# A cross-attention and mixture-of-experts layer: heads paired on the partitions, maxima added by a product, one ring of banks for the cross attention

## What is computed

```python
x = x + xattn(layernorm(x), ctx)      # 16 heads of 64; softmax kept at its 32 largest of 64 scores
y = layernorm(x)
hn = layernorm(y) * ln1_g + ln1_b
q, k, v = (hn @ w + b for w, b in ((wq, bq), (wk, bk), (wv, bv)))     # 16 heads of 16
attn = softmax(q @ k.T / sqrt(16))                                    # 512 x 512 per head
y2 = y + attn @ v @ wo + bo
hn2 = layernorm(y2) * ln2_g + ln2_b
idx = argmax(hn2 @ gate_w + gate_b)                                   # one of 8 experts
out = x + y2 + relu(hn2 @ w1[idx] + b1[idx]) @ w2[idx] + b2[idx]
```

## Time and profile before

| what | value |
|---|---|
| median of 3 runs | 1525.85 us (1525.6 to 1525.93) |
| the profiled execution's own time | 1527.39 us |
| its span in the trace | 1525.6 us |
| mean granted TensorE clock | 0.936 of full speed |
| PE busy | 1326.6 us, 87% |
| DVE busy | 1080.8 us, 71% |
| ACT busy | 705.8 us, 46% |
| POOL busy | 600.5 us, 39% |
| end of the first block (last `logits`) | 1182.1 us |

### The profile page before, as it was taken

The page is one execution under the profiler, slowest core; times in us unless marked ns, Lnnn a source line. Parts: engine busy times, 40 slices in busy tenths (PEclk is TensorE's granted clock), DMA queues, the critical chain, the costliest instruction groups (busy, mean ns, idle before and its releaser), DMA issues. The chain is left out here.

```text
span 1525.6 us, 24394 instructions
## 1 busy us (share of the span) xinstructions
PE 1326.6 (87%) x6498; PEld 878.6 (58%) x6498; DVE 1080.8 (71%) x5685; ACT 705.8 (46%) x1531; POOL 600.5 (39%) x751
## 2 busy tenths in 40 slices
PE   6756779989998998998899899899897299999996
PEld 2444346455555646555554564554434299998996
DVE  1495998999899899999989989985552622222222
ACT  2323425736654664675575457356454022222221
POOL 5035333334243324424343433341101256766663
PEclk9977889999998999999999899989998599999998
DMA  6201522163061344217125332621721446266551
GB/s 230 74 1 35 109 52 63 69 141 57 22 166 43 64 108 101 64 56 154 34 51 124 78 71 78 125 43 70 147 29 56 138 132 209 71 236 229 182 177 30
DMA packets 91946, 149.42 MB, mean 98 GB/s; under 512 B 34578, under 2 KB 43160, under 8 KB 87736
## 3 DMA queue, kind: packets, MB, share of 16 engines
q1 hardware_dynamic: 73736, 94.97, 26.4%
q0 software_dynamic: 18096, 53.19, 10.8%
HBM read 153.94 MB, written 42.86 MB: 129 GB/s over the span
## 5 line engine op out<-in xcount | busy, mean ns | idle before, releaser
L1079 DVE TENSOR_REDUCE nmax<-fr 128x1 f32<-128x512 f32 x512 | 330.0, 679 | 56.8 <-PE fr L539 56.3
L872 ACT ACTIVATE pt<-fr 128x512 f32<-128x512 f32 x512 | 276.4, 608 | 92.6 <-PE fr L539 89.9
L539 PE MATMUL fr<-ks,qs 128*128 128x512 f32 x512 | 220.9, 486 | 30.6 <-DVE nmax L1079 14.2
L539 PE MATMUL fr<-qs,ks 128*128 128x512 f32 x512 | 204.9, 477 | 20.5 <-DVE nmax L1079 12.8
L1181 POOL TENSOR_TENSOR m<-m,e 128x1024 f32<-128x1024 f32 x32 | 75.8, 2369 | 259.0 <-DVE m L1015 205.2
L539 PEld LDWEIGHTS fr<-qs,ks 128*128 128x128 f32 x512 | 97.3, 200 | 124.7 <-issue 59.9
L539 PEld LDWEIGHTS fr<-ks,qs 128*128 128x128 f32 x512 | 94.6, 197 | 108.1 <-DVE nmax L1079 48.1
L703 PE MATMUL ob<-pt,v 128*32 128x512 f32 x1024 | 139.6, 618 | 0.5 <-ACT pt L872 0.5
L539 PE MATMUL xs<-M,xnT 128*128 128x512 f32 x256 | 124.8, 611 | 1.2 <-ACT xnT L760 1.0
L539 PE MATMUL xt<-VW,pT 128*128 128x256 f32 x512 | 122.5, 394 | 2.7 <-ACT pT L760 1.3
L539 PEld LDWEIGHTS xt<-VW,pT 128*128 128x128 f32 x512 | 99.3, 198 | 19.2 <-ACT hnT L761 4.5
(11 more groups left out here) (188 smaller groups left out, 2613.0 us busy)
## 6 DMA issues: line engine op xcount, KB each, us to landing
parts_d<-parts SPq DMA_DIRECT2D x32, 512.0 KB, 3.5
qs<-parts_d SPq DMA_DIRECT2D x128, 128.0 KB, 4.1
ks<-parts_d SPq DMA_DIRECT2D x128, 128.0 KB, 5.4
xy_d<-xy SPq DMA_DIRECT2D x32, 256.0 KB, 3.6
xyf<-xy_d SPq DMA_DIRECT2D x32, 256.0 KB, 3.2
rows_d<-row SPq DMA_DIRECT2D x32, 256.0 KB, 3.2
xb<-x SPq DMA_DIRECT2D x16, 256.0 KB, 2.9
kbd<-kT_d SPq DMA_DIRECT2D x16, 128.0 KB, 3.3
```

Of the source, the lines that this page charges most:

```text
L539: return pe.matmul(o, l, r, start=first, stop=last)
L872: act.activation(pt[:, t % 2, h, :], fr_bank(b, "st", 16 * g + n)[:, :], ACT.Exp, scale=D ** -0.5)\
L1079: v.tensor_reduce(nmax[:, g % 2, 4 * h + t:4 * h + t + 1], fr_bank(b, "fs", 16 * g + n)[:, :], AX.X, ALU.max, negate=True).then_inc(fr_sig ...
```

## The change

Three things, and with them a table of due times that is new throughout.

**Heads in pairs.** `qs` and `ks` have half as many slots, and a slot holds two heads: one on partitions 0 to 63 and one on 64 to 127, 64 rows of parts each, with no row for the maximum and none of zeros. `first_pass` issues two products per step, each over 64 partitions, into the two next banks of the ring. The stack loads write the same bytes with a stride of four partitions.

**The row of maxima as a product.** `nmax` gets one column block of 72 columns per tile of queries. `max_turn` makes four transposes (72 x 128) in place of one, `max_out` copies 72 x 512 into `cB`, and the DMA of the maxima is gone (`max_load`, `cT`, `c_loaded`). `second_pass` issues four products per pair of heads: two of `ks` with `qs`, and two that add the row of maxima by a selection matrix `sel` with `cB`. `sel` is made once by DVE from the identity matrix.

**One ring of three.** `xt` joins `xs0` and `xs1`: all seven kinds of the cross attention take the three banks in turn.

Beside these, GpSimd no longer clears `qs` and `ks` (3 of its memsets), and the start's context tile lies in `pt` instead of a tile of its own.

```diff
-PERIOD = 134.36
+PERIOD = 129.07
...
-    "fs": (206.71, 206.73, 207.84, 211.36, 213.82, 217.24, 218.6, 219.6, 220.6, 222.63, 223.97, 226.38, 226.99,
...
+    "fs": (197.59, 201.66, 206.54, 209.09, 211.07, 212.91, 213.22, 213.79, 215.18, 218.79, 228.42, 229.87, 230.69,
...
-NXS, NXT, NFR = 2, 1, 4
-XS_TURN = turns("M", "VW", "sc", "pT")
-XT_TURN = turns("xt", "av", "yt")
-FR_TURN = turns("proj", "v", "fs", "ct", "st", "ot", "oT", "wo", "zT", "gt")
+NXS, NFR = 3, 4
+XS_TURN = turns("M", "VW", "sc", "pT", "xt", "av", "yt")
+FR_TURN = turns("proj", "v", "ct", "ot", "oT", "wo", "zT", "gt", pairs=("fs", "st"))
-STACK = 16 * 9
+STACK = 16 * 8
 NSLOT = 3
+NC = 64 + 2 * NT
...
-        qs = sa("qs", [P, 4 * NSLOT, S], F32R)
-        ks = sa("ks", [P, 4 * NSLOT, S], F32R)
+        qs = sa("qs", [P, 2 * NSLOT, S], F32R)
+        ks = sa("ks", [P, 2 * NSLOT, S], F32R)
+        sel = sa("sel", [P, 2, P], F32R)
+        pick_rows = sa("pick_rows", [P, 2])
...
-        nmax = sa("nmax", [P, 2, 4 * NT])
-        cT = sa("cT", [NT * 4, P], F32R)
+        nmax = sa("nmax", [P, 2, NT, NC])
+        cB = sa("cB", [P, 2, S], F32R)
...
-                    sp.dma_start(qs[D * r:D * r + D, sl, :].bitcast(F32), rows(part)).then_inc(stack_loaded[slot], 16)
+                    sp.dma_start(qs[r:P:4, sl, :].bitcast(F32), rows(part)).then_inc(stack_loaded[slot], 16)
...
-            def max_load(b):
-                for g in range(G):
-                    yield due(b, "cl", g)
-                    sl = slice(4 * SLOT[g], 4 * SLOT[g] + 4)
-                    fr_read(sp, b, "ct", g)
-                    sp.dma_start(qs[4 * D:4 * D + 1, sl, :].bitcast(F32).rearrange("o h (t c) -> o (h t) c", c=P),
-                                 cT[:, :].bitcast(F32)).then_inc(c_loaded, 16)
...
             def first_pass(b, g):
-                for n in range(16):
-                    t, h = n // 4, n % 4
-                    yield due(b, "fs", 16 * g + n)
+                for n in range(0, 16, 2):
+                    t, pair = n // 4, 2 * SLOT[g] + n % 4 // 2
+                    yield due(b, "fs", 8 * g + n // 2)
...
-                    o = fr_slot(b, "fs", 16 * g + n)
-                    mm(o[:, :], qs[:, 4 * slot + h, t * P:(t + 1) * P], ks[:, 4 * slot + h, :]).then_inc(fr_full, 1)
+                    for i in range(2):
+                        half = slice(64 * i, 64 * i + 64)
+                        o = fr_slot(b, "fs", 16 * g + n + i)
+                        mm(o[:, :], qs[half, pair, t * P:(t + 1) * P], ks[half, pair, :]).then_inc(fr_full, 1)
...
-                tr(o[0:4 * NT, 0:P], nmax[:, g % 2, :]).then_inc(fr_full, 1)
+                for t in range(NT):
+                    ins = tr(o[0:NC, t * P:(t + 1) * P], nmax[:, g % 2, t, :])
+                ins.then_inc(fr_full, 1)
...
             def second_pass(b, g):
...
                     if n == 0:
-                        pe.wait_ge(c_loaded, 16 * (G * b + g + 1))
-                    o = fr_slot(b, "st", 16 * g + n)
-                    mm(o[:, :], ks[:, sl, t * P:(t + 1) * P], qs[:, sl, :]).then_inc(fr_full, 1)
+                        fr_read(pe, b, "ct", g)
+                    halves = [slice(64 * i, 64 * i + 64) for i in range(2)]
+                    o = [fr_slot(b, "st", 16 * g + n + i) for i in range(2)]
+                    for i in range(2):
+                        mm(o[i][:, :], ks[halves[i], pair, t * P:(t + 1) * P], qs[halves[i], pair, :], True, False)
+                    for i in range(2):
+                        mm(o[i][:, :], sel[halves[i], p, :], cB[halves[i], g % 2, :], False, True).then_inc(fr_full, 1)
...
-                wait(act, c_loaded, 16 * (G * b + g))
-                copy(cT[:, :], fr_bank(b, "ct", g)[0:4 * NT, 0:P]).then_inc(fr_signal(b, "ct", g), 1)
+                last = before(b, g, 2, G)
+                if last is not None:
+                    fr_written(act, last[0], "st", 16 * last[1] + 15)
+                copy(cB[0:NC, g % 2, :], fr_bank(b, "ct", g)[0:NC, :]).then_inc(fr_signal(b, "ct", g), 1)
```

More of the change, by code:

```diff
@@ L150, in due, with turns @@
     return b * PERIOD + AT[kind][n]
-def turns(*kinds):
-    order = sorted((due(b, kind, n), b, kind, n) for b in range(B) for kind in kinds for n in range(len(AT[kind])))
+def turns(*kinds, pairs=()):
+    order = sorted((due(b, kind, n), b, kind, n) for b in range(B) for kind in kinds + pairs for n in range(len(AT[kind])))
     assert len({use[0] for use in order}) == len(order)
-    return {use[1:]: turn for turn, use in enumerate(order)}
-NXS, NXT, NFR = 2, 1, 4
-XS_TURN = turns("M", "VW", "sc", "pT")
-XT_TURN = turns("xt", "av", "yt")
-FR_TURN = turns("proj", "v", "fs", "ct", "st", "ot", "oT", "wo", "zT", "gt")
+    turn = {}
+    for _, b, kind, n in order:
+        for u in (2 * n, 2 * n + 1) if kind in pairs else (n,):
+            turn[b, kind, u] = len(turn)
+    return turn
+NXS, NFR = 3, 4
+XS_TURN = turns("M", "VW", "sc", "pT", "xt", "av", "yt")
+FR_TURN = turns("proj", "v", "ct", "ot", "oT", "wo", "zT", "gt", pairs=("fs", "st"))
 PICK_TURN = turns("tk")
-STACK = 16 * 9
+STACK = 16 * 8
 NSLOT = 3
+NC = 64 + 2 * NT
 SLOT = (0, 1, 2, 0)
@@ L314, in program @@
         pre_out = [[part[:, n:n + B * CK] for part in parts_ for n in range(0, part.shape[1], B * CK)] for parts_ in flat]
-        xs = [bank(f"xs{n}") for n in range(2)]
-        xt = bank("xt")
+        xs = [bank(f"xs{n}") for n in range(NXS)]
+        xt = xs[2]
         fr = [bank(f"fr{n}") for n in range(NFR)]
@@ L486, in stack_load @@
                 slot = SLOT[g]
-                sl = slice(4 * slot, 4 * slot + 4)
+                sl = slice(2 * slot, 2 * slot + 2)
                 last = before(b, g, 1 if g == 0 else 3 if g == 3 else 4, G)
@@ L528, in _ @@
             weave([part(b) for b in range(1, B) for part in (x_load, k_loads, v_loads)]
-                  + [part(b) for b in range(B) for part in (y_store, parts_store, max_load, xy_load, rows_store)]
+                  + [part(b) for b in range(B) for part in (y_store, parts_store, xy_load, rows_store)]
                   + [stack_load(b, g) for b in range(B) for g in range(G)])
@@ L833, in y_norm2 @@
                 if last is not None:
-                    xt_written(act, last[0], "yt", last[1])
+                    xs_written(act, last[0], "yt", last[1])
                 r = yr[:, t % 2, :]
@@ L930, in _ @@
                             ALU.mult).then_inc(consts_ready, 1)
+            for p in range(2):
+                v.tensor_reduce(pick_rows[:, p:p + 1], ident[:, :].rearrange("r (i c) -> r i c", i=2)[:, :, 4 * p:4 * p + 4],
+                                AX.XY, ALU.add).then_inc(rows_found, 1)
+            dve.wait_ge(rows_found, 2)
+            for p in range(2):
+                v.tensor_copy(sel[:, p, :], pick_rows[:, p:p + 1].to_broadcast((P, P)))
             v.tensor_scalar(bias_m[:, :], mask_u[:, :], 1.0, MASKED, ALU.subtract, ALU.mult).then_inc(consts_ready, 1)
```

134 lines of the change are left out of this document (70 added, 64 removed), and 132 rows, old and new, of the table AT.

## The result

The changed kernel takes 1561.1 us, the median of 4 runs (1559.36 to 1563.0), beside 1525.72 for the kernel before: ratio 1.0235, 95% interval 1.0217 to 1.0253. It is slower by 35 us. The prediction had 1503 in a range of 1460 to 1568, with 1544 for its first rival. The time lies in the range, but on the other side of no change: the reasoning that gave 1503 did not hold.

The account below looks back on a forecast made before the run. PE and DVE, nearly equally loaded, were taken to bound the first block together by stopping for each other. From 1525.6 us, minus 15 over 7.3 batches and minus 8 in the emptying gave 1502.6, about 1503 us; range 1460 to 1568.

Parts of the forecast that it names:

- its first rival: Whole kernel: every change of division drains and PE becomes the bound; plus 8.1 us per batch, 1544 us; chance 0.30.
- I take a third, 4.8 us: PE, per batch: share taken of the 14.4 us upper bound for 58 more division changes and second sets of weights.
- second weights: PE, 41 half-height stretches per batch: a second weight load before its product, 0.11 us each, 4.5 us together.
- The first pass: PE, per batch: 64 single products of 14.7 us become 32 side-by-side pairs of 7.4 us, minus 7.4 us.
- The sum for PE: PE, per batch: minus 7.4, plus 1.1, plus 4.8 gives minus 1.5 us, bounds minus 6.3 and plus 8.1.
- The threshold named there: First rival decides once PE's sum is no longer negative: more than 6.3 of the 14.4 us show.
- What a batch gains: Steady part: PE's minus 1.5 us and DVE getting two banks at once, together minus 2 us per batch.
- The emptying: After the last search for the 32nd score: minus 5 and minus 3 us, together minus 8 us.
- Its first term: Emptying, from the maxima's copy to the second pass: 1.1 us saved for each of six groups, five showing, minus 5.
- rival 4: First and second pass: half-height products run one after the other, plus 15.8 us per batch, about 1640 us; chance 0.06.
- the ring: Cross attention's banks, ring of three: a third bank helps, a strict turn can hurt; taken as zero.
- the filling: Start of the first block, 140 us: counted as about one batch of the 7.3 that give minus 15 us.

Follow-up runs that it names:

- the probe: Kernel before plus a 64-row, 8-column product ahead of every second first-pass product: 1574.23 us; control with 128 rows 1538.11 us.

## Why the prediction was wrong

**The step that failed** is "I take a third, 4.8 us", the share of 14.4 us for the changes of division and the second weights. The 58 changes are 7.3 us of PE's work by the probe's 0.126 us and 11.6 us by the 0.20 of the places compared; the 0.17 that the prediction had read from the 32-column group, 9.9 us in all, was a good price. The 4.5 us for second weights do not show, since the two loads run together. The reason given for a third, that a pair starts on a bank that DVE has just freed "and the array is empty then anyway", did not hold: in the probe, at the first pass's own places, the change cost PE's work all the same.

**The first pass,** minus 7.4 us, was not the mistake where it stands alone: between two 32-column groups a pair gained its 0.22 us. But half the height for the first pass also brings 37 of the changes, 7.4 us at 0.20 each. From the kernel with the first pass at full height to the changed one PE's work did not fall, it grew by 1.6 us. Up to 1.3 of that can be the clock's, 0.97 and 0.96 (an estimate, 1% of 125). The prediction set the gain and the price in separate terms and so did not see that they cancel.

**The sum for PE** depends on the price taken. At 0.20 us: first pass minus 7.4, changes plus 11.6, transposes and all the rest plus 0.6 (121.1 against 120.5) instead of 1.1, second pass minus 0.4 (the 3.8 us between the two full-height kernels, less 21 changes), close to the prediction's 0. That is plus 4.4 of the measured 6.0. At the probe's 0.126 us the second pass would be plus 1.2 and the first pass minus 3.1, which does not fit the places where it gained in full. The forecast had minus 1.5, its first rival plus 8.1. The threshold named there was that more than 6.3 of the 14.4 us show; 7.3 to 11.6 showed. Its batch of 133.2 us was measured as 134.25, against 127.7 in the forecast. Its 1544 us fell short of 1561 mainly by the emptying, where it had kept the minus 8 us.

**What a batch gains,** minus 2 us from shorter waits of DVE, became plus 4.4 us of idle time of DVE. That two banks come at once did not help enough: DVE's wait for the first pass's products grew from 23.9 to 39.6 us in five batches.

**The emptying,** minus 8 us, became plus 4.5. Its first term was right where it can be read:

```profile
1161.31 0.63 PE L526 MATMUL fr<-ident,nmax 128*72 128x128 f32 x4 [0.70 <-DVE nmax L1078]
1162.71 0.80 PE L523 MATMUL fr<-qs,ks 64*128 64x512 f32 x2 [0.31 <-ACT cB L748]
```

From the transpose of the maxima to the second pass 1.40 us instead of 2.40, minus 1.0 where 1.1 was forecast. But a group takes (1183.03 - 1121.17) / 3 = 20.6 us there instead of 16.8. DVE waits up to 9.8 us for a product of the first pass; that wait ends at 1173.47 us, behind a second pass that ran mostly at the lower clock level (the last section). The granted clock is 0.86 instead of 0.93. With both passes at full height the same table has 160 us. The forecast's 159 comes near that by luck: 3 of its minus 8 us were to come from the half-height products.

**What was right:** pairs run side by side (rival 4 is out); no price for their second set of weights shows; DVE's work stays at 121 us; the ring, the memsets and ACT's longer copy do not show as a loss (both full-height passes with the same copies and ring are below the kernel before); the second block keeps its time within 2.3 us. **What was left out:** the filling, counted as one batch of the 7.3, became 9 us shorter; it did so in all variants on the new table (first maximum at 188 to 190 us), so that is the table's. With both passes at full height the whole kernel gains 12 us by its table, its queues without the maxima and its ring, of which the ring alone gives nothing; which of the others gives it was not tried. The forecast's terms had the gain in the halved products instead.

**What stays open:** which of the moved steps makes the orders with fewer changes so much slower, and whether a table made for this purpose could put all pairs of a group together without that.

## What to carry to other kernels

Half-height products side by side pay where no new change of division comes with them. Count, from the order in which they will really be issued, the borders that are new, and price them before counting the halved time: here a border cost 0.13 to 0.20 us and a halved pair saved 0.22, so a pair that stands alone between two full-array kinds loses. The 58 new borders per batch ate the gain of the 32 pairs and more. Here, with two engines busy over 90% of a period, the one whose work grew set the period, whatever its waits had looked like before. A fitted order can be worth more than any one operation in it (96 us for twelve steps moved by up to 1 us), so compare kinds of products on one and the same order, as the full-height variants did, and not by exchanging order and product together.

## What the runs showed of the hardware that was not expected

**A change of the array's division for rows costs 0.13 to 0.20 us of PE's work,** by the probe (0.126 on average) and by places compared one by one (0.20); the same order with and without the half-height stretches accounts for the whole growth of the batch, 5.7 us.

**The granted clock depends on the kind of products.** On the same order the emptying has 0.95 and 0.96 with the first pass at full height, 0.86 with it at half height, and 0.81 without the maxima product. Over the whole program each kernel's four executions agree: 0.942 to 0.945 with the first pass at full height, 0.925 to 0.929 in the changed kernel, 0.901 to 0.907 without the maxima product. In three stretches of the changed kernel's emptying (the last column but two is the clock):

```profile
1114.00:1122.00 8.00, 7.63 (x26) 4.20 (x25) 6.70 (x14) 2.00 (x4) 1.03 (x3) 0.55 0.73 215
...
1154.00:1161.00 7.00, 5.67 (x32) 1.92 (x30) 6.52 (x12) 1.63 (x3) 0.00 (x0) 1.00 0.01 2
1161.00:1169.00 8.00, 7.22 (x30) 2.91 (x30) 2.70 (x5) 4.84 (x9) 0.00 (x0) 0.60 0.00 0
```

At 1161 to 1169 us PE is mostly at the 1.2 GHz level; before it fell it had been busy 5.67 of 7 us, at 2.4 GHz. The kernel with a full-height first pass issues the same instructions at these times and has 1.00 in both stretches:

```profile
1142.60:1149.60 7.00, 6.05 (x31) 2.24 (x30) 6.26 (x12) 1.06 (x2) 0.00 (x0) 1.00 0.00 0
1149.60:1156.00 6.40, 4.90 (x30) 2.20 (x30) 2.67 (x5) 4.46 (x9) 0.00 (x0) 1.00 0.00 0
```

There PE had been busy 6.05 of 7 us before, and what takes 8.0 us at the lower level in the changed kernel takes 6.1 here (from the transpose of the maxima at 1149.94 to the fifth pair of the second pass at 1156.05; in the changed kernel 1161.31 to 1169.31).

At the lower level the steps of the second pass are 0.56 us apart instead of 0.23 to 0.33:

```profile
1163.28 0.66 PE L523 MATMUL fr<-cB,sel 64*128 64x512 f32 x2
...
1163.84 0.79 PE L523 MATMUL fr<-qs,ks 64*128 64x512 f32 x2
```

That the half-height products are the cause is shown by the runs that differ in them alone; by what way they lower the clock is not. What it costs here is contained in the emptying's 6 us between the two kernels; the place above is 1.9 of them.

**Two half-height weight loads run together,** in 0.18 to 0.19 us at the 2.4 GHz level, where I had counted 0.11 us more for the second.
